# Multi-query attentions: where the projection of the next unit but one stands in the order of the work

## The reference, cut to what matters

```
q = (xn @ Wq).reshape(b, n, H, DH).transpose(0, 2, 1, 3) * scale
kv = xn @ Wkv                                   # one head of keys, one of values
k = concatenate([null_k, k]); v = concatenate([null_v, v])
sim = einsum('bhid,bjd->bhij', q, k) + bias     # bias: given (cond2), or by distance (cond)
sim = where(causal_mask, neg, sim); sim = where(mask, sim, neg)
out = einsum('bhij,bjd->bhid', softmax(sim), v)
out = layernorm(out.reshape(b, n, H * DH) @ Wo) * g_out
```

## Time and profile before

| | cond2_0, 7 iterations | cond1, 7 iterations | whole span |
|---|---|---|---|
| stretch, us | 1112.4 to 1709.6 | 2340.2 to 3008.5 | 0 to 4935.7 |
| PE busy | 523.45 us | 558.94 us | 4111.0 us (83%) |
| DVE busy | 385.66 us | 398.28 us | 2605.7 us (53%) |
| ACT busy | 336.31 us | 351.57 us | 1882.4 us (38%) |
| POOL busy | 50.71 us | 42.29 us | 204.6 us (4%) |
| granted TensorE clock | 0.98 | 0.96 | 0.89 |

### The profile page before, as it was taken

The page is one execution under the profiler, slowest core; times in us unless marked ns, Lnnn a source line. Parts: engine busy times, 40 slices in busy tenths (PEclk is TensorE's granted clock), DMA queues, the critical chain, the costliest instruction groups (busy, mean ns, idle before and its releaser), DMA issues. The chain is left out here.

```text
span 4935.7 us, 71449 instructions
## 1 busy us (share of the span) xinstructions
PE 4111.0 (83%) x23610; PEld 2849.2 (58%) x23610; DVE 2605.7 (53%) x6227; ACT 1882.4 (38%) x4293; POOL 204.6 (4%) x614
## 2 busy tenths in 40 slices
PE   8989999968888873457888888768888886999999
PEld 5545655555555551343555555655555565988888
DVE  3545544446666638445665655246666644443443
ACT  1124544415555512213555555025555531222221
POOL 0000000000000000000000000001000000000000
PEclk8998866879999995657999999879999996999999
DMA  1000000011112100000000000011111201001000
GB/s 33 16 9 4 2 4 2 6 52 52 67 46 72 40 9 17 8 15 9 10 11 18 10 11 15 7 53 40 63 55 51 67 9 35 18 18 35 18 18 18
DMA packets 84991, 128.61 MB, mean 26 GB/s; under 512 B 11771, under 2 KB 58883, under 8 KB 84758
## 3 DMA queue, kind: packets, MB, share of 16 engines
q1 hardware_dynamic: 84758, 125.53, 7.8%
HBM read 123.33 MB, written 2.17 MB: 25 GB/s over the span
## 5 line engine op out<-in xcount | busy, mean ns | idle before, releaser
L653 PE MATMUL ps_s<-cond_k_high,cond_q_high 128*128 128x512 f32 (+3 forms) x1152 | 477.3, 417 | 262.7 <-DVE cond_q_both L56 185.3
L689 ACT ACTIVATE cond_p<-cond_p,cond_negm 128x128 f32<-128x128 f32 (+7 forms) x768 | 590.9, 771 | 265.8 <-DVE cond_negm L727 261.9
L626 PE MATMUL ps_o<-cond_pt,cond_v 128*64 128x256 f32 (+1 forms) x3840 | 601.4, 393 | 33.5 <-DVE attn_out L759 33.5
L664 PE MATMUL ps_t<-ident,cond_p 128*128 128x128 f32 x3456 | 575.1, 286 | 0.7 <-ACT cond_pt L695 0.7
L695 ACT COPY cond_pt<-ps_t 128x512 f32<-128x512 f32 x576 | 313.5, 544 | 599.0 <-PE ps_t L664 598.7
L664 PEld LDWEIGHTS ps_t<-ident,cond_p 128*128 128x128 f32 x3456 | 405.3, 144 | 166.6 <-issue 126.1
L727 DVE CUSTOM_DVE_ANT_0 cond_p<-ps_s,cond_side,cond_null_score 128x128 f32<-128x128 f32 (+7 forms) x512 | 411.8, 817 | 158.7 <-PE ps_s L653 145.8
L653 PEld LDWEIGHTS ps_s<-cond_k_high,cond_q_high 128*128 128x128 f32 x1152 | 221.1, 192 | 472.6 <-DVE cond_q_both L56 254.8
L653 PE MATMUL ps_s<-cond_k_both,cond_q_both 128*128 128x512 f32 (+3 forms) x1152 | 395.4, 355 | 0.0
L2029 ACT ACTIVATE moe_hid<-ps_s,moe_b 128x512 f32<-128x512 f32 x256 | 176.4, 689 | 496.4 <-PE ps_s L1992 496.4
L727 DVE CUSTOM_DVE_ANT_0 attn_p<-ps_s,attn_causal 128x128 f32<-128x128 f32 (+7 forms) x272 | 201.9, 757 | 242.4 <-PE ps_s L653 240.9
(11 more groups left out here) (316 smaller groups left out, 7211.6 us busy)
## 6 DMA issues: line engine op xcount, KB each, us to landing
cond_side<-in_fside_16xSxS SPq DMA_DIRECT2D x32, 512.0 KB, 6.1
moe_w<-in_L_ffn_W SPq DMA_DIRECT2D x16, 1024.0 KB, 7.3
cond_side<-in_fside_16xSxS SPq DMA_DIRECT2D x32, 448.0 KB, 5.3
cond_side<-in_fside_16xSxS SPq DMA_DIRECT2D x32, 384.0 KB, 4.9
cond_side<-in_fside_16xSxS SPq DMA_DIRECT2D x32, 320.0 KB, 4.3
cond_side<-in_fside_16xSxS SPq DMA_DIRECT2D x32, 256.0 KB, 3.4
cond_toep<-distance_bias SPq DMA_DIRECT2D x16, 512.0 KB, 4.3
cond_side<-in_fside_16xSxS SPq DMA_DIRECT2D x32, 192.0 KB, 3.1
```

What stands on the lines that cost most here:

```text
L626: last = nc.tensor.matmul(m.O[n % 2][h * W:(h + 1) * W, s0 * P:PH * P], a.values(h, b, kb), PT[c % PTS][:, (h * PH + s0) * P:(h + 1) * PH ...
L653: last = nc.tensor.matmul(bank(it, n, EX + r)[:, lo:hi], x, y, start=(i == 0), stop=(i == len(parts) - 1))
L664: last = nc.tensor.transpose(m.T[c % 2][:, r * P:(r + 1) * P], Pr[n % 2][r][:, kb * P:(kb + 1) * P], m.ident[:, :])
L689: nc.scalar.activation(p, p, ACT.Exp, bias=negm[n % 2][:, r:r + 1], scale=-1.0, accum_out=rsum[n % 2][:, r:r + 1]).then_inc(exped, 1)
```

## The change: what it does

Within unit n, `proj n+2` moves from the start to just behind the step of the last row of unit n+1, ahead of the chunk of that block; `halves n+2` moves one block behind it, to after that block's chunk and `attend`. So the projection now stands in block 0 in A, in block 1 in B, in block 3 in C and in block 4 in D. In `first_steps` the second projection and its halves move behind the rows and exponentials of unit 0. `use` is rewritten for the new order: the projection of a unit is now taken directly before its rows.

```diff
         steps.append(("null", n))
+        project = ahead and n + 2 < end
         halves = None
-        if ahead and n + 2 < end:
-            steps.append(("proj", n + 2))
-            halves = ("halves", n + 2)
         placed = 0
         for kb in range(blocks):
             late = []
...
                 placed += 1
+            if halves is not None:
+                late.append(halves)
+                halves = None
+            if project and placed == len(rows):
+                steps.append(("proj", n + 2))
+                halves = ("halves", n + 2)
+                project = False
             steps.append(("chunk", n, kb, chunk))
...
             if kb == 0:
                 steps.append(("den", n))
-            if halves is not None:
-                steps.append(halves)
-                halves = None
             steps += ends.pop(chunk, [])
             chunk += 1
+        if halves is not None:
+            steps.append(halves)
...
-    steps = [("proj", 0), ("halves", 0), ("proj", 1), ("halves", 1)]
+    steps = [("proj", 0), ("halves", 0)]
     for r in range(R):
         steps += [("row", 0, r), ("exp", 0, r)]
+    steps += [("proj", 1), ("halves", 1)]
     return steps
...
-        if k < EX:
-            at_ = n * (EX + R) - R if n else 0
-        else:
-            at_ = n * (EX + R) + EX + k
-            if EX == 0 or n == U - 1 and isinstance(it, int) and it == a.iters - 1:
-                at_ -= EX
-        return it * UPI + at_ + 1
+        return it * UPI + n * (EX + R) + k + 1
```

## The result

The changed kernel is slower: 5006.94 us (median of four runs, 4999.05 to 5014.94) against 4946.88 us, a ratio of 1.0122 with a 95% interval of 1.0102 to 1.0142. The profiled execution took 5006.15 us, its span is 5004.4 us. I forecast slower, 4968 us, with a range up to 4995: the direction was right, the size (+60 us) three times mine.

What follows compares the result with a forecast made beforehand. TensorE sets the pace, so its idle time decides. Two cond2 stages lose 29.4 us and cond1 gains 11.0, together +18; 4937.6 becomes 4956, and with the median 11.7 above that, 4968 us, range 4940 to 4995.

Steps and rivals of the forecast that it cites:

- A: Two-block unit, first of a half iteration: waits at rows 1 and 3 shrink; gain .91 us in cond2, .7 in cond1.
- B: Four-block unit after A: first `attend` waits behind the later cut; about 1.5 us longer in cond2, +.2 in cond1.
- C: Six-block unit: row 1's wait goes, but the halves delay the next unit's first row; +.45 us in cond2, -.1 in cond1.
- D: Eight-block unit: row 1's wait goes, a new wait for a copied chunk comes; -.1 us in both cond2 and cond1.
- The clock: TensorE's clock in the three changed stages: taken as unchanged, since waits become fewer but longer.
- my own 10 us: Smallest difference a measurement can tell from no change: .2%, about 10 us.
- The price of a fall: Time TensorE loses at 1.2 GHz in the three stages of the kernel before: at most 58 us in all.
- Rival 4: At the end of A, the 2.6 us wait makes one more clock fall in each of 24 iterations: +38, 5006 us; chance .12.
- Rival 1: From A's first row to its last chunk the clock stays up: up to 58 us, half gives 4939 us; chance .17.
- Rival 2: Waits simply go, VectorE and ScalarE having slack: 2.9 us a half in cond2, 4.5 in cond1; 165, 4784 us; chance .04.
- Rival 3: Two sides balance: B costs 1.2, C nothing, D -.3, cond1 takes back 11: 4940 to 4958, say 4950 us; chance .16.

Runs made afterwards that it cites:

- the filled kernel before: Kernel before plus unused matmuls, six ahead of the bank wait at A's row 1, five ahead of B's first row: 4895.3 us, ratio 0.9915.
- the last two versions: Changed kernel with A's halves early and B's projection in block 2, halves early: 4769.74 us; with C's halves early, D's projection in block 5, halves early: 4715.72 us.

## Why the prediction was right in its sign and wrong in its size

**The order at full clock: right in cond2, too little gain in cond1.** For cond2 I had A -.91, B +1.5, C +.45, D -.1, sum +.94. The half without a fall shows -.77, +1.68, +.23, -.24, sum +.90. For cond1 I had -.7, +.2, -.1, -.1, sum -.7. Against the 46.70 of the filled kernel before it is -.73, +.15, -.31, -.37, sum -1.25. The units that I had wrong are C and D. C's wait for the halves is .44 and not .7: the copy ahead of them ended 4.73 behind the fourth row, as I had it, but the next row came at 5.63 and not 5.7, and the head of C won .36 and not .25. D's wait for the chunk is .57 and not .8, because the cut ended 3.35 behind the fourth row and not 3.5, and TensorE asked for the bank a little later. These are the copy and the row in C (its fourth row is at 1294.34), the end of the cut and the chunk in D (fourth row at 1305.43):

```profile
1298.49 0.58 ACT L694 COPY cond_pt<-ps_t 128x512 f32<-128x512 f32 x1
...
1299.97 0.33 PE L652 MATMUL ps_s<-cond_k_high,cond_q_high 128*128 128x128 f32 x1 [0.44 <-ACT cond_q_high L1361]
...
1308.35 0.43 DVE L56 TENSOR_TENSOR cond_q_both<-ps_s,cond_q_both 64x256 fp32r<-64x256 f32 x1
...
1309.56 0.66 PE L663 MATMUL ps_t<-ident,cond_p 128*128 128x128 f32 x4 [0.57 <-DVE cond_pt L734]
```

Over the stages: 2 x (15 x .90 + .91) - (15 x 1.25 + .57) = 28.8 - 19.3 = +9.5, where I had +18.

**The clock: the step that failed.** It was "The new order makes fewer waits, but longer ones, so I take no change": a term put at nothing, for which the sentence gives no reason. From the means of the halves, cond2 lost .45 us a half to falls before (42.35 against 41.90) and 1.44 after (44.24 against 42.80); cond1 1.31 (48.01 against 46.70) and 2.83 (48.28 against 45.45). That is 32 x .99 + 16 x 1.52 = +56 (cond2_0 stands for both cond2 stages). With +9.5 it makes +66; the medians differ by 60 and the two spans by 69. By stage it is +30, +5 and +30. From the first row of a stage to the end of its last B the two traces differ by +31.5, +5.9 and +33.8, so what lies outside doesn't explain the loss. The numbers for a better judgement stood in the prediction: 2.6 us without work at the end of every A, where a fall had followed waits of 1.70 and .46. A fall behind it costs 1.58 (B 12.19 against 10.61); in the kernel before one in A cost 1.26, because it also shortened B's wait, from 1.59 to .84.

**Luck.** "Slower" came true by the term that I had put at nothing. The order that I did work out is worth +9.5, which my own 10 us would hardly tell from no change.

**The price of a fall** was also known only as a bound (58 us in all stages). The filled kernel before gives back 43. By the halves the falls cost 35 us in the kernel before (32 x .45 + 16 x 1.31) and 91 in the changed one (32 x 1.44 + 16 x 2.83).

**Rivals.** Rival 4 had the mechanism, a fall more behind the wait of 2.6, and I gave it .12. It had +38, up to 1.6 in each of 24 iterations; the falls cost +56, 2.0 more an iteration in cond2 and 3.0 in cond1, where the output's wait of 2.12 makes a second one. Its 5006 lies within 1 us of the measurement because its +18 was too much and its +38 too little. Rival 1 (the clock stays up) was wrong as to this change, but its price was real: the fillings give it back. Rival 2 (the waits simply go) fell on the output in B, as argued. For cond1 it had 4.5 a half, less than the four waits of its own rows (2.23 + 1.63 + .75 + 1.36 = 5.97). That it names what the move can bring is shown by the last two versions, once the halves and the cut stand where little waits behind them. Rival 3 needed B at 1.2; it was 1.68. The Trainium skill's rule on idle gaps (TensorE: Matmul & The Clock Gate, section on HAM oscillation), by which no fall would come behind waits as short as these, does not hold here: falls follow single waits of 2.45 us in cond2 and 2.12 in cond1, and the first rows of B run at full clock when the first wait is filled (.51) or shortened to 1.16 (.50).

**What stays open.** Why a fall follows a wait in some halves and not in others: the wait of 2.45 is followed by none in one half of cond2_0 and one of cond1, and with A's wait filled half of cond2_0 is free of falls while cond2_1 has one in nearly every C, behind the same 1.70.

## What to carry to other kernels

A step that is moved off one queue's path lands in another queue: list for every engine what now stands behind each of its instructions and who waits for that, and choose the block in which nobody does. Merging several short waits of TensorE into one long one can cost more than the order gains, so price a wait with its fall (here 1.3 to 1.6 us), and test it by filling the wait with unused matmuls. When a good move measures slower, read its new waits before dropping it: those of A and B, put right, turned +1.2% into -3.1%.

## What the runs showed of the hardware that I had not expected

Ten unused 128x512 matmuls in a wait of 2.45 us made the changed kernel faster, and eleven made the kernel before .85% faster (0.9885 to 0.9945). The falls lock to the loop: in the changed kernel eleven halves in a row are 44.37 us long to within .03, each with one fall in the same place, while the kernel before had one in about every second half of cond2 and in every half of cond1. A single wait of TensorE of 2.45 us was enough, though not in every half.
